# A state-space scan kernel in which GpSimd multiplies two channel tiles with one instruction

## The chip, the cores and the metric

The kernel runs on one core of one Trainium2 chip. The metric is the device time of one execution in microseconds (us); lower is better. The core has a tensor engine (PE in the profile, its weight loads PEld), a vector engine (DVE), a scalar engine (ACT), GpSimd (POOL) and a sync engine (SP) that issues most transfers. Each engine runs its own list of instructions in order, and they wait for each other through semaphores.

## The reference

An input `x` of 4 sequences of 1024 tokens with 256 features is layer-normalised to `xn`. Two things are made of `xn`: a mixture of 8 experts of which each token uses one, and a stack of 8 Mamba layers. The output is `x + s * silu(g)`, with `s` from the Mamba stack and `g` from the experts. The change lies in the Mamba layers, whose core is this recurrence over time, for 512 channels and 16 states:

```python
def _mamba_layer(x, Wi, cw, cb, Wx, Wdt, bdt, Alog, Dp, Wo):
    xz = jnp.einsum('bld,ed->ble', x, Wi)
    xin, z = jnp.split(xz, 2, axis=-1)
    xin = _silu(_causal_conv(xin, cw, cb))
    x_dbl = jnp.einsum('blc,ec->ble', xin, Wx)
    ...
    delta = jax.nn.softplus(jnp.einsum('blr,cr->blc', dt_raw, Wdt) + bdt)
    A = -jnp.exp(Alog)
    y = _selective_scan(delta, Bm, Cm, xin, A, Dp)
    y = y * _silu(z)
    return jnp.einsum('blc,dc->bld', y, Wo)

def step(h, inp):          # one token of _selective_scan
    d_t, B_t, C_t, u_t = inp
    h = h * jnp.exp(d_t[..., None] * A) + (d_t * u_t)[..., None] * B_t[:, None, :]
    y = jnp.einsum('bcn,bn->bc', h, C_t)
    return (h, y)
```

The term `(d_t * u_t) * B_t` is the drive of the recurrence. It is what the change is about.

## The kernel before

**Stages.** `experts` normalises and runs the mixture, `mamba` runs the 8 layers, `finish` combines both. `mamba` takes nearly the whole time.

**Units and tiles.** `mamba` works in 64 units: 8 layers times 4 sequences times 2 halves of 512 tokens. Channels lie on the 128 partitions, so the 512 channels are 4 tiles (index `j`), and time runs along the free dimension. A unit loops over 16 states (`n`) and the 4 channel tiles, which makes 64 tiles of 128x512 float32, numbered `k = 4n + j`. Units with even number U hold the first half of a sequence and start their states at 0; odd ones start them from `carry`, the last column of the unit before.

**One tile.** For tile `k`
- ACT (`exponent`, L784) writes the decay `exp(delta * A)` to `ps_d`, two buffers in PSUM;
- GpSimd (L743) writes `drive[k % 8] = du[j] * brep[n]`. `du` (`delta * u`, 4 tiles) is made once per unit by DVE in two instructions of two tiles each (`make_du`, L978, after tiles 58 and 63 of the unit before). `brep` is B of one state, spread over all partitions by a DMA, with 4 buffers;
- DVE (`scan`, L930) runs the recurrence over the 512 tokens with one TENSOR_TENSOR_SCAN of `ps_d` (in PSUM) and `drive` (in SBUF);
- PE transposes the state (L1085), ACT weighs it with C (L791, `prod`), PE transposes it back and adds it into `ps_y` (L1092).

**What holds GpSimd back.** The semaphore `scanned` counts scans and `drive_set` counts tiles of drive. There are 8 drive buffers, so tile `k` may be written once scan `k - 8` has ended (`scanned >= 64 U + k + 1 - DRIVE`, L742). Between the drives GpSimd has small work at fixed places: `keep_carry` (in even units after tile 4n + 9, waits for scan 4n + 3), `set_taps` after tile 16, `halo` after tile 17 (waits for the convolution step that DVE does after scan 14), `set_cur` after tile 20, `mask_x` (L705, two rows of 512 at once, one operand repeated) after tile 23, `set_skip` (L722, four small instructions) after tile 30.

**What DVE does between the scans.** The order is written out by hand as pairs (n, j), "after the scan of this tile": `CONV_AT`, `SOFT_AT`, `DU_AT`, `MARK_AT`, `ALIVE_AT`, `ADD_AT`. As tile numbers of the unit:
- convolution, 16 steps (L965 the first of each four, L969 the others): after tiles 7, 9, 12, 14, 14, 30, 33, 37, 39, 46, 47, 50, 52, 55, 59, 63; L965 is at 9, 30, 46 and 55;
- softplus, 8 steps of two tiles each: L988 after 27 and 35, L991 after 28 and 42, L995 after 29 and 60, L998 after 31 and 61;
- `make_du` (L978) after 58 and 63;
- marks of overflow: L939 after 6, L941 after 8; a scan of them (L952) after 10;
- `gate` (L1028) after tiles 4 to 7 and `add_x` (L1034) after 14 and 15, with one operand in PSUM each.

**PE and ACT.** Besides the transposes PE runs the projections, through a ring of two PSUM banks whose order is written out in `RING_AT`. ACT does both SiLUs of a unit after tile 15 (`SILU_AT`).

Of the kernel before, what the change touches and what calls it, by code (L numbers as in the profile page):

```python
# [27 lines left out]
ALU = mybir.AluOpType  # L28
# [3 lines left out]
P = 128  # L32
# [3 lines left out]
T = 512  # L36
# [32 lines left out]
TILES = STATES * CB  # L69
XD = RANK + 2 * STATES  # L70
BREP = 4
DRIVE = 8
# [410 lines left out]
def items_before(U, kind):  # L483

    if kind == "mid":
        every, vec = U * len(ITEMS["mid"]) + PRE_ALL, U * len(BY_DVE["mid"]) + PRE_DVE
        return every, vec, U * (len(ITEMS["mid"]) - len(BY_DVE["mid"])) + PRE_ALL - PRE_DVE
    past = ORDER[:ORDER.index(kind)]
    every, vec = sum(len(ITEMS[k]) for k in past), sum(len(BY_DVE[k]) for k in past)
    return every, vec, every - vec  # L490
# [22 lines left out]
def item_read(U, kind, name):  # L513

    i = ITEMS[kind].index(name)
    act, vec = reads(U, kind, i + 1)
    return vec if name in VEC_ITEMS else act
# [13 lines left out]
def mamba(nc, w_in, w_x, w_dt, w_out, par, xres, ident, alive_dram, bc_dram):  # L531

    with ExitStack() as ctx:
# [31 lines left out]
        du = sb("du", [P, CB, T])  # L565

        brep = sb("brep", [P, BREP, T])
        drive = sb("drive", [P, DRIVE, T])
# [20 lines left out]
        drive_set, decay_set, scanned, carried = sem("drive_set"), sem("decay_set"), sem("scanned"), sem("carried")  # L589
# [3 lines left out]
        def is_first(U):  # L593
            return isinstance(U, int) and U == 0

        def units(eng, unit):

            unit(0, 0, 0, "first")
            unit(1, 1, 0, "mid")
            with nc.Fori(1, ITERS - 1, 1, engines=[eng.engine], hint_back_edge=True) as it:  # L600
                for h in range(HALVES):
                    unit(HALVES * it + h, h, it, "mid")
            unit(UNITS - 2, 0, ITERS - 1, "near")
            unit(UNITS - 1, 1, ITERS - 1, "last")
# [76 lines left out]
        @block.gpsimd  # L681
        def _(pool):
            def wait_counted(semaphore, count):

                pool.wait_ge(semaphore, count)
                pool.sem_inc(pool_waited, 1)

            def set_cur(F, h, it):

                if not (isinstance(F, int) and F < 2):  # L690
                    wait_counted(scanned, TILES * (F - 1))
                nc.gpsimd.tensor_copy(cur[h][:], params[:, bass.ds(it // BATCH, 1), :].rearrange("p a c -> p (a c)")).then_inc(cur_set, 1)

            def set_taps(G, h, it):

                if not (isinstance(G, int) and G < 2):
                    wait_counted(conv_done, CB * (G - 1))
                nc.gpsimd.tensor_copy(taps[h][:], params[:, bass.ds(it // BATCH, 1), COL_W:COL_DT].rearrange("p a c -> p (a c)")).then_inc(taps_set, 1)

            def mask_x(U, kind, G, h, it):  # L700
                pool.wait_ge(ring_vec, item_read(U, kind, "CNT"))
                if not (isinstance(G, int) and G < 2):

                    pool.wait_ge(ring_ready, items_before(U, kind)[0])
                nc.gpsimd.tensor_tensor(xm[h][:], xres[:, :, bass.ds((it % BATCH) * SEQ + h * T, T)],  # L705
                                        alive[h][:].unsqueeze(1).to_broadcast([P, DB, T]), ALU.mult).then_inc(xm_set, 1)

            def halo(F, h):

                wait_counted(conv_done, CB * F + CB)  # L710
                if h == 0:
                    nc.gpsimd.tensor_copy(xpad[:, :, 0:TAPS - 1], xpad[:, :, T:T + TAPS - 1]).then_inc(halo_set, 1)
                else:
                    nc.gpsimd.memset(xpad[:, :, 0:TAPS - 1], 0.0).then_inc(halo_set, 1)

            def set_skip(F, h):

                if not is_first(F):
                    wait_counted(skip_used, F)
                wait_counted(cur_set, F + 1)  # L720
                for j in range(CB):
                    last = nc.gpsimd.tensor_scalar(skip[:, j, :], ident[:], cur[h][:, COL_D + j:COL_D + j + 1], 1.0,  # L722
                                                   ALU.mult, ALU.mult)
                last.then_inc(skip_set, 1)

            def keep_carry(U, n):

                wait_counted(scanned, TILES * U + CB * n + CB)
                nc.gpsimd.tensor_copy(carry[:, n, :], state[n % 2][:, :, T - 1]).then_inc(carried, 1)  # L729

            def unit(U, h, it, kind):
                F, hf, itf = U + 1, 1 - h, it + h
                G, itg = U + 2, it + 1
                for n in range(STATES):
                    for j in range(CB):
                        k = CB * n + j
                        if j == 0:
                            pool.wait_ge(brep_in[n % BREP], 16 * (STATES // BREP * U + n // BREP + 1))
                        if n == 0 and j % 2 == 0:
                            pool.wait_ge(du_set, 2 * U + j // 2 + 1)  # L740
                        if not (is_first(U) and k < DRIVE):
                            pool.wait_ge(scanned, TILES * U + k + 1 - DRIVE)  # L742
                        nc.gpsimd.tensor_tensor(drive[:, k % DRIVE, :], du[:, j, :], brep[:, n % BREP, :],  # L743
                                                ALU.mult).then_inc(drive_set, 1)
                        if h == 0 and k >= CARRY_LAG and k % CB == CARRY_LAG % CB:
                            keep_carry(U, (k - CARRY_LAG) // CB)
                        if h == 1 and k + TILES - CARRY_LAG < TILES and (k + TILES - CARRY_LAG) % CB == 0:
                            keep_carry(U - 1, (k + TILES - CARRY_LAG) // CB)
                        if kind != "last":
                            if (n, j) == CUR_AT:  # L750
                                set_cur(F, hf, itf)
                            if (n, j) == HALO_AT:
                                halo(F, hf)
                            if (n, j) == SKIP_AT:
                                set_skip(F, hf)
                        if kind in ("first", "mid"):
                            if (n, j) == TAPS_AT:
                                set_taps(G, h, itg)
                            if (n, j) == XM_AT:
                                mask_x(U, kind, G, h, itg)  # L760

            nc.gpsimd.memset(xdbl[:], 0.0).then_inc(xdbl_clear, 1)
            nc.gpsimd.memset(xpad[:, :, 0:TAPS - 1], 0.0).then_inc(halo_set, 1)
            pool.wait_ge(par_set, 1)
            set_cur(0, 0, 0)
            set_taps(0, 0, 0)
            set_taps(1, 1, 0)
            mask_x(0, "pre0", 0, 0, 0)
            set_skip(0, 0)
            halo(0, 0)  # L770
            mask_x(0, "pre1", 1, 1, 0)
            units(pool, unit)

        @block.scalar
# [590 lines left out]
```

## Time and profile before

| | |
|---|---|
| median of 3 runs | 8067.98 us (8058.57 to 8072.14) |
| the profiled execution | 8078.57 us, its span 8076.8 us |
| DVE busy | 85% of the span |
| PE busy | 84% |
| ACT busy | 80% |
| GpSimd (POOL) busy | 76% |
| tensor engine's mean granted clock | 0.971 of full |

The profiled execution is 0.13% above the median. Its span runs from the first to the last instruction, and 1.8 us of its time lie outside. All durations in this document come from that one execution unless a comparison of runs is named. An engine's "busy" time includes the time that an instruction, once issued, spends blocked.

### The profile page before, as it was taken

To read this page: it belongs to the slowest core of one execution; us is meant where nothing else is said; L and a number is where in the kernel's file an instruction comes from. 1 tells how busy PE (TensorE), PEld (TensorE's weight loads), DVE (VectorE), ACT (ScalarE), POOL (GpSimd) and SP (SyncE) were. 2 spreads that over 40 slices of the span, in tenths; PEclk is the share of its full clock that TensorE was granted. 3 is DMA by queue.
4 is the path that set the end of the run, shared out by engine and by line. 5 is a ranking of instruction groups with operands and counts; after the bars stand their busy time and mean duration, and the time that the engine had idled before them with its cause. 6 is when DMAs were issued, how large, how long until landed. Compare 5 with 4: busy or idle time off the path is not lost. (4 is left out here: it accounts for less than half of the span.)

```text
span 8076.8 us, 143189 instructions
## 1 busy us (share of the span) xinstructions
PE 6817.6 (84%) x39539; PEld 4773.9 (59%) x39539; DVE 6885.2 (85%) x6710; ACT 6451.8 (80%) x10242; POOL 6100.4 (76%) x5283
## 2 busy tenths in 40 slices
PE   4978888888888888888888888888888888888887
PEld 3645655655665656556555655665565566556655
DVE  2249889988988898889889988988998898889888
ACT  1248888888888888888888888888888888888886
POOL 2137877887888788888877887887788778878875
PEclk9989999999999999999999999999999999999998
DMA  5111111111111111111111111111111111111112
GB/s 167 34 33 38 38 35 44 41 38 37 41 40 40 38 38 41 42 38 38 38 42 40 38 38 38 41 40 36 37 44 41 38 37 40 41 39 38 37 37 88
DMA packets 205422, 348.52 MB, mean 43 GB/s; under 512 B 24976, under 2 KB 63664, under 8 KB 204496
## 3 DMA queue, kind: packets, MB, share of 16 engines
q1 hardware_dynamic: 201216, 329.67, 15.2%
q0 software_dynamic: 3408, 9.33, 0.3%
q8 instruction: 364, 5.96, 0.3%
q14 instruction: 434, 3.56, 0.1%
HBM read 318.04 MB, written 20.88 MB: 42 GB/s over the span
## 5 line engine op out<-in xcount | busy, mean ns | idle before, releaser
L743 POOL TENSOR_TENSOR drive<-du,brep 128x512 f32<-128x512 f32 x4096 | 5610.7, 1396 | 856.1 <-DVE du L978 641.1
L784 ACT ACTIVATE ps_d<-delta,cur 128x512 f32<-128x512 f32 x4096 | 2827.0, 690 | 867.1 <-DVE state L930 846.3
L1085 PE MATMUL ps_r<-ident,state 128*128 128x128 f32 x16384 | 2575.0, 281 | 565.1 <-ACT prod L791 338.6
L791 ACT ACTIVATE prod<-ps_r,bcT 128x512 f32<-128x512 f32 x4096 | 2784.7, 680 | 262.5 <-PE ps_r L1085 250.8
L930 DVE TENSOR_TENSOR_SCAN state<-ps_d,carry,drive 128x512 f32<-128x512 f32 x2048 | 2518.9, 1265 | 274.9 <-ACT ps_d L784 138.1
L930 DVE TENSOR_TENSOR_SCAN state<-ps_d,drive 128x512 f32<-128x512 f32 x2048 | 2394.1, 1205 | 280.2 <-ACT ps_d L784 139.4
L1092 PE MATMUL ps_y<-ident,prod 128*128 128x128 f32 x16384 | 2508.6, 278 | 27.6 <-ACT prod L791 25.4
L1085 PEld LDWEIGHTS ps_r<-ident,state 128*128 128x128 f32 x16384 | 1867.4, 143 | 878.3 <-ACT prod L791 558.0
L1092 PEld LDWEIGHTS ps_y<-ident,prod 128*128 128x128 f32 x16384 | 1960.3, 143 | 694.5 <-issue 489.1
L1125 PE MATMUL ps_r<-xm,w_inx_sb 128*128 128x512 f32 x1024 | 534.3, 648 | 189.6 <-ACT prod L791 181.9
L969 DVE SCALAR_TENSOR_TENSOR xc<-xpad,taps,xc 128x512 f32<-128x512 f32 x768 | 657.4, 856 | 2.9
L1133 PE MATMUL ps_r<-xm,w_inz_sb 128*128 128x512 f32 x1024 | 510.0, 621 | 126.0 <-ACT prod L791 125.8
L1162 PE MATMUL ps_r<-relu,w_out_sb 128*128 128x512 f32 x1024 | 471.6, 604 | 5.6 <-ACT prod L791 3.0
L1125 PEld LDWEIGHTS ps_r<-xm,w_inx_sb 128*128 128x128 f32 x1024 | 180.2, 195 | 384.3 <-issue 198.5
L1155 PE MATMUL ps_r<-xdbl,w_dt_sb 16*128 16x512 f32 x512 | 299.9, 666 | 84.2 <-ACT soft L837 51.4
L1133 PEld LDWEIGHTS ps_r<-xm,w_inz_sb 128*128 128x128 f32 x1024 | 174.6, 190 | 312.7 <-ACT prod L791 169.1
L729 POOL COPY carry<-state 128x4 f32<-128x4 f32 x512 | 189.7, 371 | 182.1 <-DVE state L930 179.6
L1162 PEld LDWEIGHTS ps_r<-relu,w_out_sb 128*128 128x128 f32 x1024 | 185.3, 191 | 202.2 <-issue 189.0
L1103 PE MATMUL ps_y<-u,skip 128*128 128x512 f32 x512 | 283.8, 692 | 23.5 <-DVE relu L1028 23.5
L1141 PE MATMUL ps_r<-u,w_x_sb 128*48 128x512 f32 x512 | 234.9, 602 | 54.4 <-ACT u L809 54.4
L425 ACT ACTIVATE hid<-ps_t,b_sb 128x128 f32<-128x128 f32 x312 | 84.8, 382 | 227.4 <-PE ps_t L386 227.4
L353 POOL DMA_INDIRECT ys_dram<-yb,row x39 | 37.2, 955 | 294.4 <-DVE yb L445 294.4
(136 smaller groups left out, 4471.4 us busy)
## 6 DMA issues: line engine op xcount, KB each, us to landing
brep<-bc_dram SPq DMA_DIRECT2D x1024, 256.0 KB, 3.3
w_sb<-w SPq DMA_DIRECT2D x8, 1024.0 KB, 17.9
w_all<-w SPq DMA_DIRECT2D x8, 1024.0 KB, 13.0
xs_dram<-nothing SPq DMA_DIRECT2D x1, 5011.5 KB, 35.0
xb<-xs_dram SPq DMA_DIRECT2D x39, 128.5 KB, 2.0
w_all<-x SPq DMA_DIRECT2D x1, 4096.0 KB, 14.7
w_inx_sb<-w_in SPq DMA_DIRECT2D x8, 512.0 KB, 4.0
w_inz_sb<-w_in SPq DMA_DIRECT2D x8, 512.0 KB, 4.0
```

The lines of the kernel that those rows point to most:

```text
L743: nc.gpsimd.tensor_tensor(drive[:, k % DRIVE, :], du[:, j, :], brep[:, n % BREP, :], ALU.mult).then_inc(drive_set, 1)
L784: nc.scalar.activation(ps_d[:, k % 2, :], delta[h][:, j, :], ACT.Exp, scale=cur[h][:, a:a + 1]).then_inc(decay_set, 1)
L791: nc.scalar.activation(prod[:, t, :], ps_r[:, item_place(U, h, kind, item), :], ACT.Copy, scale=bcT[(h + 1) % 2 if item[1] == "prev" else ...
L930: nc.vector.tensor_tensor_scan(state[n % 2][:, j, :], ps_d[:, k % 2, :], drive[:, k % DRIVE, :], carry[:, n, j:j + 1] if h == 1 else 0.0, ...
L969: step = nc.vector.scalar_tensor_tensor(xc[:, j, :], xpad[:, j, tap:tap + T], w, xc[:, j, :], ALU.mult, ALU.add)
L1085: last = nc.tensor.transpose(out[:, j * P:(j + 1) * P], state[n % 2][:, j, t * P:(t + 1) * P], ident[:])
L1092: last = nc.tensor.matmul(ps_y[:, j, t * P:(t + 1) * P], prod[:, t, j * P:(j + 1) * P], ident[:], start=False, stop=True, is_transpose=Tru ...
L1103: last = nc.tensor.matmul(ps_y[:, j, :], skip[:, j, :], u[:, j, :], start=True, stop=True, skip_group_check=True)
L1125: last = nc.tensor.matmul(out, w_inx_sb[:, k, j * P:(j + 1) * P], xm[h][:, k, :], start=(k == 0), stop=(k == DB - 1))
L1133: last = nc.tensor.matmul(out, w_inz_sb[:, k, j * P:(j + 1) * P], xm[hf][:, k, :], start=(k == 0), stop=(k == DB - 1))
L1155: nc.tensor.matmul(out, w_dt_sb[:, j * P:(j + 1) * P], xdbl[0:RANK, :], start=True, stop=True).then_inc(ring_ready, 1)
L1162: last = nc.tensor.matmul(out, w_out_sb[:, j, k * P:(k + 1) * P], gated[:, j, :], start=(j == 0), stop=(j == CB - 1))
```

## The change

GpSimd makes the products of channel tiles `j` and `j + 1` (for even `j`) with one TENSOR_TENSOR of 2 x 512 elements per partition. Its second operand, the row of `brep`, is repeated for both with stride 0. There are 32 such instructions per unit in place of 64. Each waits until both of its buffers are free, and counts `drive_set` up by 2 when it ends. The small work of GpSimd keeps its places in the loop, so what stood between two tiles of a pair now stands behind the pair.

```diff
--- before.py
+++ after.py
@@ -738,10 +738,11 @@
                             pool.wait_ge(brep_in[n % BREP], 16 * (STATES // BREP * U + n // BREP + 1))
                         if n == 0 and j % 2 == 0:
                             pool.wait_ge(du_set, 2 * U + j // 2 + 1)
-                        if not (is_first(U) and k < DRIVE):
-                            pool.wait_ge(scanned, TILES * U + k + 1 - DRIVE)
-                        nc.gpsimd.tensor_tensor(drive[:, k % DRIVE, :], du[:, j, :], brep[:, n % BREP, :],
-                                                ALU.mult).then_inc(drive_set, 1)
+                        if j % 2 == 0:
+                            if not (is_first(U) and k < DRIVE):
+                                pool.wait_ge(scanned, TILES * U + k + 2 - DRIVE)
+                            nc.gpsimd.tensor_tensor(drive[:, k % DRIVE:k % DRIVE + 2, :], du[:, j:j + 2, :],
+                                                    brep[:, n % BREP:n % BREP + 1, :].to_broadcast([P, 2, T]), ALU.mult).then_inc(drive_set, 2)
                         if h == 0 and k >= CARRY_LAG and k % CB == CARRY_LAG % CB:
                             keep_carry(U, (k - CARRY_LAG) // CB)
                         if h == 1 and k + TILES - CARRY_LAG < TILES and (k + TILES - CARRY_LAG) % CB == 0:
```

## Rows read from the trace of the kernel before

**Rows 1.** The page: the span and each engine's busy time.
```profile
span 8076.8 us, 143189 instructions
PE 6817.6 (84%) x39539; PEld 4773.9 (59%) x39539; DVE 6885.2 (85%) x6710; ACT 6451.8 (80%) x10242; POOL 6100.4 (76%) x5283
```

**Rows 2.** The waits over the span: us in total, times, longest.
```profile
POOL drive L743 <- DVE du L978: 641.1, 126, 7.2
...
DVE state L930 <- ACT ps_d L784: 277.5, 199, 6.1
...
POOL drive L743 <- DVE state L930: 154.0, 145, 4.7
...
DVE state L930 <- POOL drive L743: 42.1, 26, 1.8
```

**Rows 3.** One line's instructions each: duration in ns, min/median/max; six lines.
```profile
L743 POOL TENSOR_TENSOR drive<-du,brep x4096: 1250/1274/2293, 531.7 to 8001.4; 128x512 f32<-128x512 f32 x196
...
L705 POOL TENSOR_TENSOR xm<-xres,alive x64: 2337/2370/2394, 476.5 to 7727.0; 128x1024 f32<-128x1024 f32 x64
...
L969 DVE SCALAR_TENSOR_TENSOR xc<-xpad,taps,xc x768: 717/799/1844, 484.0 to 7834.5; 128x512 f32<-128x512 f32 x192
...
L965 DVE TENSOR_SCALAR xc<-xpad,taps x256: 514/598/1602, 483.4 to 7826.2; 128x512 f32<-128x512 f32 x128
...
L991 DVE TENSOR_TENSOR low<-soft,low x128: 1192/1399/3756, 509.4 to 7887.1; 128x1024 f32<-128x1024 f32 x128
...
L1028 DVE TENSOR_TENSOR relu<-ps_y,zs x256: 657/666/693, 671.2 to 8016.1; 128x512 f32<-128x512 f32 x128
```

**Rows 4.** Timeline of POOL in an even unit: start, us, what.
```profile
4096.39 4.99 POOL L743 TENSOR_TENSOR drive<-du,brep 128x512 f32<-128x512 f32 x4
...
4110.40 3.72 POOL L743 TENSOR_TENSOR drive<-du,brep 128x512 f32<-128x512 f32 x3
4116.41 2.17 POOL L743 TENSOR_TENSOR drive<-du,brep 128x512 f32<-128x512 f32 x1 [2.30 <-DVE state L930]
```

**Rows 5.** Timeline of DVE in the same unit.
```profile
4111.46 3.74 DVE L991 TENSOR_TENSOR low<-soft,low 128x1024 f32<-128x1024 f32 x1
...
4116.25 1.19 DVE L995 TENSOR_TENSOR low<-low,delta 128x1024 f32<-128x1024 f32 x1
...
4136.53 1.53 DVE L991 TENSOR_TENSOR low<-soft,low 128x1024 f32<-128x1024 f32 x1
4137.98 4.55 DVE L930 TENSOR_TENSOR_SCAN state<-ps_d,drive 128x512 f32<-128x512 f32 x4
4142.46 1.07 DVE L965 TENSOR_SCALAR xc<-xpad,taps 128x512 f32<-128x512 f32 x1
```

**Rows 6.** Timeline of DVE in the odd unit behind it.
```profile
4189.73 1.52 DVE L965 TENSOR_SCALAR xc<-xpad,taps 128x512 f32<-128x512 f32 x1
...
4253.58 1.39 DVE L991 TENSOR_TENSOR low<-soft,low 128x1024 f32<-128x1024 f32 x1
4254.89 4.79 DVE L930 TENSOR_TENSOR_SCAN state<-ps_d,carry,drive 128x512 f32<-128x512 f32 x4
4259.61 0.65 DVE L965 TENSOR_SCALAR xc<-xpad,taps 128x512 f32<-128x512 f32 x1
```

**Rows 7.** Timeline at the change of units: DVE.
```profile
4170.41 1.20 DVE L978 TENSOR_TENSOR du<-delta,u 128x1024 f32<-128x1024 f32 x1
4171.53 0.74 DVE L969 SCALAR_TENSOR_TENSOR xc<-xpad,taps,xc 128x512 f32<-128x512 f32 x1
4172.19 4.80 DVE L930 TENSOR_TENSOR_SCAN state<-ps_d,carry,drive 128x512 f32<-128x512 f32 x4
```

**Rows 8.** The same moment: POOL.
```profile
4171.77 5.32 POOL L743 TENSOR_TENSOR drive<-du,brep 128x512 f32<-128x512 f32 x4 [6.90 <-DVE du L978]
```

**Rows 9.** Windows, an even and an odd unit: us, then each engine's busy time.
```profile
4055.40:4171.50 116.10, 101.20 (x597) 70.18 (x596) 104.54 (x100) 99.04 (x155) 94.38 (x87) 0.97 0.16 43
4171.50:4288.00 116.50, 100.27 (x592) 70.48 (x590) 104.87 (x100) 98.51 (x155) 94.12 (x73) 0.97 0.14 38
```

## The prediction

> **What bounds the kernel now.** I read the page first: no engine is full; DVE is busiest with 85%, GpSimd has 76% [rows 1]. The windows of two neighbouring units say that a unit takes 116.3 us, of which DVE is busy 104.5 to 104.9 and GpSimd 94 [rows 9]. The waits come next. GpSimd waits 641 us for `du`, about 10 us per unit, and 154 us for scans; DVE waits for a drive in only 26 places, 42 us in all [rows 2]. So GpSimd runs ahead, and making it faster shortens no wait that DVE has for it. DVE's own large wait is for the decay, 277.5 us [rows 2]; it falls after the two SiLUs, between tiles 15 and 26. From tile 27 to 63, and from 0 to 14, DVE works nearly without a gap. There DVE sets the pace: a microsecond more in one of its instructions is a microsecond more per unit.
>
> The third view, durations by line, holds what decides. `gate` (one operand in PSUM) takes 657 to 693 ns always, while L969, L965 and L991 go from 717, 514 and 1192 ns to 1844, 1602 and 3756 [rows 3]. The timelines of both engines show why. L991 is issued at 4111.46, inside a run of three drives that ends at 4114.12. It ends at 4115.20, so its own 1.19 us began at 4114.01, when those drives were over [rows 3 to 5]. The reverse stands 2 us later: L995 is issued at 4116.25, a drive at 4116.41; the drive takes 2.17 us and ends 1.13 us behind L995's end of 4117.44 [rows 4, 5]. So a DVE instruction with two operands in SBUF, or a TENSOR_SCALAR out of SBUF, and a GpSimd product exclude each other, and the later one waits until the earlier is over. Scans, gates and `add_x`, with an operand in PSUM, don't wait. I call the others port instructions; a unit has 28 of them (16 of the convolution, 8 softplus, 2 `du`, 2 marks).
>
> Here is what the wait costs now. A wait is a duration less the line's minimum. In the even unit I find 0.2 to 0.6 us at single places (0.34 on L991 after tile 42, 0.56 on L965 after tile 46) [rows 3, 5], and 2.55 once, after tile 28, where L991 sat through three drives. Over the whole unit that is 6.1 us. In the odd unit it is 2.9 us, of which 1.0 after tile 9 and 0.2 on L991 after tile 42 [rows 3, 6]. They are so small because the lengths fit: a drive takes 1.25 us (four in 4.99) [rows 4], a scan 1.12 us from start to start in even units (four in 4.48) [rows 5] and 1.18 in odd ones (4254.89 to 4259.61) [rows 6]. When DVE comes back for the port after one, two or three scans, a drive is just ending.
>
> **The change part by part.**
>
> *Fewer, longer instructions.* The trace has one of the new form, `mask_x`: 1024 elements, one operand repeated, 2.37 us [rows 3]. Two drives in a row take 2.50 [rows 4]. So a pair costs 2.37, with two drives as the upper bound, and GpSimd saves 0.13 x 32 = 4 us per unit. This is worth nothing by itself: it goes into GpSimd's waits for scans.
>
> *Both buffers must be free.* Pair (k, k+1) waits for scan k-7, an odd one. It is ready about 2.4 us later, while scan k is 6 scans (over 6.7 us) away. This is free in the steady part. Carry copies stay behind the same tiles and in time.
>
> *Start of a unit.* The pair (2, 3) can't start before the second `du`. Today GpSimd starts at 4171.77, is blocked by L969 until 4172.27, and makes four drives until 4177.09; scans 0 and 1 run from 4172.19 [rows 7, 8]. New: the pair ends about 2.2 us after 4172.27, at 4174.5. Scan 2 wants it at 4172.19 + 2 x 1.18 = 4174.55 in odd units, and 0.1 us earlier in even ones. I take 0, bound 0.2 us; the cover is scans 0 and 1.
>
> *The port.* This is the term that counts. GpSimd now waits for odd scans, so in the full part of the unit it starts a pair when an odd scan ends and keeps the port over the next two scans (2.37 us against 2.24 or 2.36). A port instruction behind an odd tile comes just as the pair ends: DVE goes first, wait 0 to 0.2. One behind an even tile comes in the middle of a pair. It waits 2.37 - 1.12 (or 1.18), less some 0.1 for the early hand-over, so 1.1; where the pair itself was late or a copy came before it, up to 1.4. Behind even tiles stand 6, 8, 12, 14, 14, 28, 30, 42, 46, 50, 52, 58, 60. At 12 and 14 GpSimd is idle before `halo`, at 58 and 60 it waits for `du`; after 59 the pair (0, 1) of the next unit, started by the first `du`, is in the way. I walked both kinds of unit from scan to scan:
> - Even unit, new waits: after 6 0.75, 7 0.4, 8 1.3, 27 0.3, 28 1.15, 30 1.1, 33 and 37 0.15 each, 42 1.3, 46 1.45, 50 1.3, 52 1.3, 55 0.1, 59 1.0. Sum 11.75, less today's 6.1: +5.65. After 28 it gains: GpSimd has only one pair allowed there, not three drives.
> - Odd unit: after 6 0.65, 7 0.3, 8 0.95, 9 0, 27 0.1, 28 and 30 0.95 each, 42 and 46 1.15 each, 50 and 52 1.1 each, 55 0.1, 59 1.0. Sum 9.5, less 2.9: +6.6.
>
> Mean 6.1 us per unit, times 64: 390 us. DVE's idle time in these parts that could soak it up is 0.2 us per unit, left out. PE and ACT have more slack when DVE slows. Against the profiled span that is 8076.8 + 390 = 8467. The median of the runs lies 10 us under the profiled execution: 8068 + 390 = 8458, I say 8460.
>
> The Trainium skill (SBUF — State Buffer, "Who interferes with whom") states that GpSimd and such DVE instructions share a port pair as an exclusive lock, held for the whole instruction. By that rule a 1024-element product blocks for all its length, which is the case forecast here, 8460; a port that came free between the two rows would give the first rival's 8010 instead. The trace agrees for 512 elements; no run here yet shows it for 1024 elements. The wait over three drives [rows 4, 5] is longer than that rule alone gives.
>
> **Rivals.**
> - *Faster: the port comes free between the two rows of a pair.* Then waits at single places stay near today's 0.2 to 0.6 us, and the one of 2.55 us after tile 28 falls, as GpSimd may be only one pair ahead there. It decides if the mean port wait at even tiles stays under 0.4 us. Price: -1.4 to -2.5 us in 32 even units, -45 to -80: 8010. For it speaks only that `mask_x` never met a port instruction, so 1024 elements aren't seen. Chance 0.08.
> - *Nothing moves:* the waits shift but sum up alike, within 0.2%: 8068. With 6 to 7 even places per unit it would take chance. 0.04.
> - *Only the late pair:* the port is as the first rival has it, and DVE waits at the start of each unit for a pair that ends one drive later: 1.1 us x 64 = 70, 8140. Against it stands that DVE waits for a drive only 42 us today, and scans 0 and 1 cover. Chance 0.06.
> - *DVE loses the port more often.* After tile 28 it asked 0.1 us before a drive ended and lost two further hand-overs. With pairs and scans nearly equally long such close calls may come at each odd tile (27, 33, 37, 55). Each costs a whole pair, 2.3 us x 64 = 147 us: 8610 with one per unit, 8750 with two. Against it: at most odd tiles GpSimd isn't yet allowed its next pair. Chance 0.12.
> - *My forecast*, 0.70: own range 8320 to 8560. The low end has the even places at 0.7 of my wait (4 us per unit, +255); the high end adds a lost hand-over in every second or third unit.
>
> **How the numbers follow.** The time is the likeliest case's, 8460. The range leaves out the cases at or under 8140 (0.18) and the top of the last rival (0.03): 8200 to 8640. A measurement of this kernel can tell about 0.2% (16 us) from no change. Slower by more: 0.70 + 0.12 + 0.06 = 0.88; within: 0.04; faster: 0.08.
>
> **What would show it.** In the profile after: L743 x2048 at 2.37 us minimum, GpSimd's unblocked work down, its waits for scans up from 154 us; L991 at two clear lengths, near 2.1 to 2.5 after tiles 28 and 42; L965 after 30 and 46 at 1.4 to 2.0 and after 9 and 55 at 0.5 to 0.7; L969 after 50 and 52 near 1.9; L941, 0.66 today, near 1.6 to 2.0; scans and gates unchanged; the unit 122 to 123 us. I am wrong if L965 and L969 keep their medians, if a unit's DVE gains idle time for drives of over 0.5 us, or if pairs take more than 2.5 us unblocked.

## The result and the profile after

The changed kernel takes 8469.06 us (median of 4 runs, 8461.93 to 8473.27) against 8070.06 us of the kernel before in the same comparison. The ratio is 1.0495, 95% interval 1.0476 to 1.0513: 4.9% slower. The profiled execution has a span of 8471.5 us. In the changed kernel's file the lines behind L743 are one higher: the product is L744, the scan L931, the convolution L966 and L970, softplus L989, L992, L996 and L999, the marks L940 and L942.

First the page, its span and busy times, beside [rows 1]:

```profile
span 8471.5 us, 141141 instructions
PE 6905.9 (82%) x39475; PEld 4785.2 (56%) x39539; DVE 7284.9 (86%) x6710; ACT 6467.2 (76%) x10242; POOL 5572.9 (66%) x3235
```

GpSimd is 527 us less busy with its products in 2048 instructions, DVE is 400 us more busy with the same 6710 instructions. The span grew by 395 us. So the time sits inside DVE's instructions, not between them. Five of the six lines of [rows 3], duration in ns as min/median/max, and the second mark (L942, after tile 8):

```profile
L744 POOL TENSOR_TENSOR drive<-du,brep x2048: 2340/2367/3205, 528.4 to 8396.2; 128x1024 f32<-128x1024 f32 x187
...
L970 DVE SCALAR_TENSOR_TENSOR xc<-xpad,taps,xc x768: 715/742/2721, 478.4 to 8228.5; 128x512 f32<-128x512 f32 x192
...
L966 DVE TENSOR_SCALAR xc<-xpad,taps x256: 514/636/2035, 477.8 to 8220.3; 128x512 f32<-128x512 f32 x128
...
L992 DVE TENSOR_TENSOR low<-soft,low x128: 1225/2290/2698, 506.1 to 8283.1; 128x1024 f32<-128x1024 f32 x128
...
L942 DVE TENSOR_SCALAR over_mark<-xres x64: 683/1658/1868, 466.5 to 8090.8; 128x1024 bf16 x60, 128x1024 bf16<-128x1024 f32 x4
...
L1029 DVE TENSOR_TENSOR relu<-ps_y,zs x256: 656/664/693, 671.6 to 8412.5; 128x512 f32<-128x512 f32 x128
```

A pair takes 2.37 us, as forecast. Note the convolution: its median fell from 799 to 742 ns, while its maximum rose. Most of its steps stand behind odd tiles and wait less than before; a few wait a whole microsecond more. A median alone would have hidden the loss, and the prediction's sign "wrong if L965 and L969 keep their medians" was a poor one for that reason: they went from 598 to 636 and from 799 to 742 ns. The gate, with an operand in PSUM, is unchanged.

The place decides, and the timeline of DVE in an even unit shows it (tiles 37 to 47: start, us, what):

```profile
4076.86 0.74 DVE L970 SCALAR_TENSOR_TENSOR xc<-xpad,taps,xc 128x512 f32<-128x512 f32 x1
4077.53 2.32 DVE L931 TENSOR_TENSOR_SCAN state<-ps_d,drive 128x512 f32<-128x512 f32 x2
4079.77 0.72 DVE L970 SCALAR_TENSOR_TENSOR xc<-xpad,taps,xc 128x512 f32<-128x512 f32 x1
4080.42 3.43 DVE L931 TENSOR_TENSOR_SCAN state<-ps_d,drive 128x512 f32<-128x512 f32 x3
4083.78 2.56 DVE L992 TENSOR_TENSOR low<-soft,low 128x1024 f32<-128x1024 f32 x1
4086.26 4.55 DVE L931 TENSOR_TENSOR_SCAN state<-ps_d,drive 128x512 f32<-128x512 f32 x4
4090.74 2.03 DVE L966 TENSOR_SCALAR xc<-xpad,taps 128x512 f32<-128x512 f32 x1
4092.70 1.21 DVE L931 TENSOR_TENSOR_SCAN state<-ps_d,drive 128x512 f32<-128x512 f32 x1
4093.83 0.72 DVE L970 SCALAR_TENSOR_TENSOR xc<-xpad,taps,xc 128x512 f32<-128x512 f32 x1
```

And GpSimd at the same time:

```profile
4080.51 4.75 POOL L744 TENSOR_TENSOR drive<-du,brep 128x1024 f32<-128x1024 f32 x2
4087.64 0.19 POOL L729 COPY carry<-state 128x4 f32<-128x4 f32 x1 [2.38 <-DVE state L931]
4087.79 4.70 POOL L744 TENSOR_TENSOR drive<-du,brep 128x1024 f32<-128x1024 f32 x2
```

Behind the odd tiles 37, 39 and 47 the convolution takes 0.72 to 0.74 us. L992 follows tile 42: issued at 4083.78, it ends at 4086.34, so its own 1.19 us began at 4085.15, 0.1 us before the second pair ended at 4085.26. L966 follows tile 46 and ends at 4092.77, so its own 0.51 us began at 4092.26, 0.23 us before the pairs ended at 4092.49. And GpSimd now idles, because pairs wait for scans (the waits, us in total, times, longest; beside [rows 2]):

```profile
POOL drive L744 <- DVE state L931: 895.1, 683, 7.8
POOL drive L744 <- DVE du L979: 692.7, 124, 8.9
...
DVE state L931 <- ACT ps_d L785: 286.7, 195, 6.1
```

The forecast went place by place, so it can be checked so. Waits in us, the mean over units 5 to 61 of the duration less the line's minimum in the kernel before. The table has the port instructions with 0.15 us or more somewhere, and the sum is that of all:

```
even unit, after tile    6    7    8   27   28   30   33   37   42   46   50   52   59   sum
before                 .59  .58    0  .36 1.98  .12  .27  .17  .34  .56  .29  .38  .22   6.20
forecast               .75  .40 1.30  .30 1.15 1.10  .15  .15 1.30 1.45 1.30 1.30 1.00  11.75
after                  .67  .40 1.20  .26  .98  .94  .03  .03 1.36 1.51 1.29 1.46 1.37  11.72

odd unit, after tile     6    7    8    9   27   28   30   42   46   50   52   59        sum
before                   0  .49    0 1.01  .26    0    0  .20  .14  .13    0  .16        3.07
forecast               .65  .30  .95    0  .10  .95  .95 1.15 1.15 1.10 1.10 1.00        9.50
after                  .48  .34  .99    0  .14  .91  .88 1.30 1.19 1.23 1.24 1.31       10.12
```

A unit lasts 123.48 us in place of 117.00 (means over the same units). The waits make 6.3 us of the 6.5. The first five units and the last two grow by less, so the span grows by 395 us and not by 64 x 6.5 = 415.

### The profile page after: what moved, and what is told of

Same layout as the page of the kernel before. It is cut to its first block and busy times, and to the rows that moved or that the text cites. A ratio compares the mean times of both kernels' runs of the same rounds, so it can differ in the third digit from the quotient of the medians.

```text
span 8471.5 us, 141141 instructions
## 1 busy us (share of the span) xinstructions
PE 6905.9 (82%) x39475; PEld 4785.2 (56%) x39539; DVE 7284.9 (86%) x6710; ACT 6467.2 (76%) x10242; POOL 5572.9 (66%) x3235
## 5 line engine op out<-in xcount | busy, mean ns | idle before, releaser
L744 POOL TENSOR_TENSOR drive<-du,brep 128x1024 f32<-128x1024 f32 x2048 | 5062.6, 2481 | 1609.3 <-DVE state L931 895.1
L931 DVE TENSOR_TENSOR_SCAN state<-ps_d,carry,drive 128x512 f32<-128x512 f32 x2048 | 2519.6, 1265 | 255.4 <-ACT ps_d L785 134.2
L931 DVE TENSOR_TENSOR_SCAN state<-ps_d,drive 128x512 f32<-128x512 f32 x2048 | 2398.0, 1204 | 304.9 <-ACT ps_d L785 152.5
L970 DVE SCALAR_TENSOR_TENSOR xc<-xpad,taps,xc 128x512 f32<-128x512 f32 x768 | 834.5, 1087 | 2.9
L1134 PE MATMUL ps_r<-xm,w_inz_sb 128*128 128x512 f32 x1024 | 542.6, 656 | 192.7 <-ACT prod L792 192.4
L992 DVE TENSOR_TENSOR low<-soft,low 128x1024 f32<-128x1024 f32 x128 | 296.4, 2316 | 0.1
L966 DVE TENSOR_SCALAR xc<-xpad,taps 128x512 f32<-128x512 f32 x256 | 276.3, 1079 | 13.7 <-ACT xpad L798 13.7
```

Of the source, the lines that this page charges most:

```text
L744: nc.gpsimd.tensor_tensor(drive[:, k % DRIVE:k % DRIVE + 2, :], du[:, j:j + 2, :], brep[:, n % BREP:n % BREP + 1, :].to_broadcast([P, 2, T ...
L931: nc.vector.tensor_tensor_scan(state[n % 2][:, j, :], ps_d[:, k % 2, :], drive[:, k % DRIVE, :], carry[:, n, j:j + 1] if h == 1 else 0.0, ...
L970: step = nc.vector.scalar_tensor_tensor(xc[:, j, :], xpad[:, j, tap:tap + T], w, xc[:, j, :], ALU.mult, ALU.add)
L992: nc.vector.tensor_tensor(low[:], soft[:, pair, :], low[:], ALU.subtract).then_inc(soft_step, 1)
L1134: last = nc.tensor.matmul(out, w_inz_sb[:, k, j * P:(j + 1) * P], xm[hf][:, k, :], start=(k == 0), stop=(k == DB - 1))
```

## The experiments

All compare with runs of the kernel before on the same chip. The theory is the one of the prediction: GpSimd's product and DVE's port instructions exclude each other, and a port instruction that meets a pair in its middle waits for its end.

**e1: two halves.** The pair's wait stays, its product becomes two instructions:

```diff
-    nc.gpsimd.tensor_tensor(drive[:, k % DRIVE:k % DRIVE + 2, :], du[:, j:j + 2, :], ...).then_inc(drive_set, 2)
+    nc.gpsimd.tensor_tensor(drive[:, k % DRIVE, :], du[:, j, :], brep[:, n % BREP, :], ALU.mult).then_inc(drive_set, 1)
+    nc.gpsimd.tensor_tensor(drive[:, k % DRIVE + 1, :], du[:, j + 1, :], brep[:, n % BREP, :], ALU.mult).then_inc(drive_set, 1)
```

> The pair's wait (both buffers free) is kept, but its product is made by two instructions of 512 elements, one right behind the other. Port theory: DVE can take the port between the halves, so the waits of the port instructions fall from the changed kernel's 1.0 to 1.4 us behind even tiles back to 0.1 to 0.4; 7980 to 8100 us. Rival, the coarse signal (GpSimd starts later because two buffers must be free, and drives come later): the time stays near the changed kernel's 8470, at least above 8350.

Measured: 8102.63 us, ratio 1.0047 (1.0030 to 1.0064), 2.6 us above the top of the theory's interval and far from the rival's 8350. Its convolution and L992 (here L971 and L993), by line:

```profile
L971 DVE SCALAR_TENSOR_TENSOR xc<-xpad,taps,xc x768: 718/752/1639, 483.4 to 7861.0; 128x512 f32<-128x512 f32 x192
...
L993 DVE TENSOR_TENSOR low<-soft,low x128: 1198/1530/2509, 508.7 to 7912.8; 128x1024 f32<-128x1024 f32 x128
```

The waits after 42, 46, 50 and 52 are back at 0.34, 0.56, 0.29 and 0.38 us in even units, to the hundredth those of the kernel before. Elsewhere e1 isn't the kernel before: 1.0 us more after tile 30 in both kinds of unit and 0.9 more after 28 in odd ones, 1.5 less after 28 in even ones. Summed, its waits are 5.2 and 4.5 us per unit against 6.2 and 3.1, which is 0.2 us more in the mean; another 0.2 is idle time of DVE, before tiles 23 and 24. So of the 399 us some 360 belong to the length of the instruction, and some 40 to the later start. The rival falls.

**e2: the other phase.** Each pair waits for one scan more and starts when an even scan ends:

```diff
-    pool.wait_ge(scanned, TILES * U + k + 2 - DRIVE)
+    pool.wait_ge(scanned, TILES * U + k + 3 - DRIVE)
```

> The changed kernel, each pair waiting for one scan more, so that GpSimd starts it when an even scan ends. Port theory: what decides is where a port instruction falls within the pair. Behind even tiles (42, 46, 50, 52) the waits fall from over 1.0 to below 0.3 us, behind odd ones (27, 29, 31, 33, 35, 37, 39, 47, 55) they rise from 0 to 0.2 to about 1.1; more places are odd than even in that stretch, so 8450 to 8600 us. Rival, the longer instruction costs its wait at random, whatever the phase: the same places keep their waits and the time stays within 0.3% of 8470.

Measured: 8676.87 us, ratio 1.0751 (1.0733 to 1.0768), 77 us above the top of the theory's interval. The direction and the places are its own. L999 follows tiles 31 (in the way of a pair now) and 61 (not), and its two durations part:

```profile
L999 DVE TENSOR_TENSOR delta<-low,relu x128: 1191/1224/2575, 511.9 to 8517.1; 128x1024 f32<-128x1024 f32 x128
```

In even units the waits after 42, 46, 50 and 52 fall from 1.3 to 1.5 us to 0.24, 0.14, 0.18 and below 0.1; those after 29, 31, 33, 35, 37, 39 and 55 rise from below 0.15 to 1.05 to 1.35. Against the expectation, after 27 it is 0.2 us and not 1.1; after 28 it stays at 1.1. The waits of a unit sum to 3.3 us more than in the changed kernel, and the unit is 3.3 us longer. The same instruction at the same length costs 200 us more or less, by its phase alone.

**e8: the cost doubled.** From the second state on one product of 4 x 512 elements:

```diff
-    if j % 2 == 0: ... pool.wait_ge(scanned, TILES * U + k + 2 - DRIVE) ... [P, 2, T] ... .then_inc(drive_set, 2)
+    w = 2 if n == 0 else 4
+    if j % w == 0: ... pool.wait_ge(scanned, TILES * U + k + w - DRIVE) ... [P, w, T] ... .then_inc(drive_set, w)
```

> The suspected cost doubled: from the second state on, one product of 4 x 512 elements, started when a scan 4m+3 ends and 4.7 us long. Port theory: a port instruction waits 3.4 us behind a tile 4m, 2.3 behind 4m+1, 1.2 behind 4m+2, 0 to 0.2 behind 4m+3; L991 after 28 takes 4.6, L969 after 33 and 37 3.0, after 52 4.1, L998 after 31 1.2. With some idle time for late drives 9000 to 9300 us. Rival, a port instruction waits at most for one row of 512 or a fixed time: 8500 or less.

Measured: 9361.17 us, ratio 1.161 (1.1591 to 1.1629), 61 us above the interval. The product's median (2048 elements) and the convolution's maximum:

```profile
L745 POOL TENSOR_TENSOR drive<-du,brep x1088: 2343/4537/5387, 528.1 to 9280.7; 128x2048 f32<-128x2048 f32 x160, 128x1024 f32<-128x1024 f32 x22
...
L971 DVE SCALAR_TENSOR_TENSOR xc<-xpad,taps,xc x768: 718/1659/4871, 480.4 to 9111.3; 128x512 f32<-128x512 f32 x192
```

The waits in even units are 3.5 us after 52 (tile 4m), 2.1 and 2.0 after 33 and 37 (4m+1), 1.0, 1.2 and 0.9 after 42, 46 and 50 (4m+2), about 0 after 35, 39 and 55. The expectation had 3.4, 2.3, 1.2 and 0 to 0.2. After 28 it is 2.75, less than expected, and after 7 4.0, where 0 to 0.2 was expected. A port instruction waits for the rest of whatever product is running. The waits of a unit sum to about 21.6 and 20.7 us, some 16.5 more than in the kernel before in the mean; the unit is 20.7 us longer, and most of the rest is idle time of DVE (3.9 us, 1.2 of it before the gate of tile 4).

**e5: four instructions moved by one tile.** The changed kernel with L992 of tile 42 behind 43, and the convolution of 46, 50 and 52 behind 45, 51 and 53:

```diff
-CONV_AT = [..., (11, 2), (11, 3), (12, 2), (13, 0), ...]
+CONV_AT = [..., (11, 1), (11, 3), (12, 3), (13, 1), ...]
-SOFT_AT = [(6, 3), (7, 0), (7, 1), (7, 3), (8, 3), (10, 2), (15, 0), (15, 1)]
+SOFT_AT = [(6, 3), (7, 0), (7, 1), (7, 3), (8, 3), (10, 3), (15, 0), (15, 1)]
```

> The changed kernel with four port instructions moved by one tile, from behind tiles 42, 46, 50 and 52 to 43, 45, 51 and 53, nothing else. Their waits in the changed kernel sum to 5.6 us per even and 5.0 per odd unit. Port theory: these waits go almost wholly (0 to 0.1 left each), no others come, 64 x 5.0 = 320 us: 8150, between 8120 and 8200. Rival after e3, the waits only hide ACT's and PE's own limit and come back as DVE's idle time: 8300 or more.

Measured: 8165.06 us, ratio 1.0126 (1.0109 to 1.0143), 15 us from the forecast. Four entries in a table take back 300 of the 400 us. 0.25 us is left after 43, 0.19 after 51 in even units, 0.13 or less in odd ones.

**e3 and e4: all of them odd.** All port instructions of tiles 27 to 63 stand behind odd tiles, the marks both behind 7; e3 with pairs, e4 with the kernel before's products:

```diff
-CONV_AT = [(7, 2), (8, 1), (9, 1), (9, 3), (11, 2), (11, 3), (12, 2), (13, 0), (13, 3), (14, 3), (15, 3), ...
-DU_AT = [(14, 2), (15, 3)]
+CONV_AT = [(9, 1), (9, 3), (10, 1), (11, 1), (11, 3), (12, 1), (12, 3), (13, 1), (13, 3), (14, 1), (14, 3), ...
+DU_AT = [(14, 3), (15, 3)]
-MARK_AT, ALIVE_AT, ADD_AT = [(1, 2), (2, 0)], ...
-SOFT_AT = [(6, 3), (7, 0), (7, 1), (7, 3), (8, 3), (10, 2), (15, 0), (15, 1)]
+MARK_AT, ALIVE_AT, ADD_AT = [(1, 3), (1, 3)], ...
+SOFT_AT = [(6, 3), (7, 1), (7, 3), (8, 1), (8, 3), (10, 3), (15, 1), (15, 1)]
```

> The changed kernel, with DVE's port instructions of tiles 27 to 63 and the two marks moved behind odd tiles (which scan each follows, nothing else). Port theory: all of them then come as a pair ends, their waits sum to 1 to 2.5 us per unit in place of 10.6 and fall below those of the kernel before (4.5), so 7830 to 7950 us, faster than both kernels. Rival, pairs are too coarse for DVE in any order (lost hand-overs, a drive that comes late): 8200 or more, with waits of over 1 us behind odd tiles too. A convolution or softplus step that now comes too late for ACT or PE would show as new idle time of DVE at tiles 0 to 26.

> The kernel before (64 products of 512 elements) with DVE's instructions at the same odd places as e3: the control for e3. Port theory: with drives of 1.25 us against scans of 1.12 or 1.18 two scans fall 0.15 to 0.25 us short of two drives, so each place waits 0.1 to 0.3 us, a sum of 3 to 5 us, as before; the wait of 2.55 us at tile 28 may vanish. 7980 to 8070 us, so e3 beats it by 1% or more. Rival, the moved places alone make the gain: e4 is as fast as e3 within 0.3%.

Measured: e3 8218.64 us (1.0191, 1.0174 to 1.0208), e4 8240.84 (1.0222, 1.0205 to 1.0239). Both expectations missed, e3 by 269 us and e4 by 171, counted from the top of each interval; e3's time is that of its rival. What the theory says of the places came true: behind all odd tiles from 29 to 63 e3 has waits below 0.1 us, and only 0.26 and 0.14 after 27. What undid it stands elsewhere. The three port instructions behind tile 7 wait 3.4 us together in even units and 3.2 in odd ones; DVE then idles 1.1 us before the scan of marks at tile 10 and 0.4 to 0.8 before tile 12; and 0.8 to 1.5 us of new idle time stands before tiles 31 and 32. e4 shares the waits behind tile 7 (2.3 and 3.2 us) and the idle time before tiles 10 and 12 (1.5 us together), but has only 0.3 to 0.4 before 31 and 32, and waits 2.0 us after 29 in even units. The two lie 0.3% apart, so with these places pairs and single products lose alike: the places made this loss, if not by the same waits in both.

**e6 and e7: near the old places.** Fewer moves: L992 28 to 29 (where L996 stands already), L966 30 to 31 (where L999 stands), the convolution of 59 to 57, four moved as in e5, the marks behind 1 and 3; e6 with pairs, e7 without.

```diff
+CONV_AT = [(7, 3), (8, 1), (9, 1), (9, 3), (11, 1), (11, 3), (12, 3), (13, 1), (13, 3), (14, 1), (15, 3), ...
+MARK_AT, ALIVE_AT, ADD_AT = [(0, 1), (0, 3)], ...
+SOFT_AT = [(6, 3), (7, 1), (7, 1), (7, 3), (8, 3), (10, 3), (15, 0), (15, 1)]
```

> Pairs, with each port instruction behind an odd tile or where GpSimd idles, but close to its old place, so that tiles 27 to 31 aren't thinned out as in e3: four moved as in e5, L991 28 to 29, L965 30 to 31, the convolution of 59 to 57, the marks to tiles 1 and 3, where DVE idles 0.8 us before the first gate. Port theory: 10 to 11 us per unit less than the changed kernel, 7780 to 7850. Rival (ACT and PE take over as limits): idle time of DVE before the scans of tiles 28 to 40 grows by over 1 us per unit and the time stays above 7950.

> The kernel before with DVE's instructions at the places of e6: its control. Port theory: singles keep waits of 0.1 to 0.3 us at most places, some 3 us per unit, and save the marks' idle time: 7900 to 8020, above e6. If it ties with e6 the longer instruction is worth nothing even where it fits.

Measured: e6 8330.35 us (1.0333, 1.0316 to 1.0350), e7 8114.09 (1.0063, 1.0046 to 1.0080). Both missed, e6 by 480 us and e7 by 94, counted from the top of each interval. e6 didn't miss by its rival's way: there is no new idle time before tiles 28 to 40. The timeline of DVE shows what I had done (odd unit, two port instructions behind tile 29, two behind 31):

```profile
4100.70 1.20 DVE L992 TENSOR_TENSOR low<-soft,low 128x1024 f32<-128x1024 f32 x1
4101.94 3.27 DVE L996 TENSOR_TENSOR low<-low,delta 128x1024 f32<-128x1024 f32 x1
4105.12 2.45 DVE L931 TENSOR_TENSOR_SCAN state<-ps_d,carry,drive 128x512 f32<-128x512 f32 x2
4107.49 1.19 DVE L999 TENSOR_TENSOR delta<-low,relu 128x1024 f32<-128x1024 f32 x1
4108.61 2.59 DVE L966 TENSOR_SCALAR xc<-xpad,taps 128x512 f32<-128x512 f32 x1
```

and of GpSimd:

```profile
4100.93 3.19 POOL L744 TENSOR_TENSOR drive<-du,brep 128x1024 f32<-128x1024 f32 x1 [0.39 <-DVE state L931]
4107.71 3.20 POOL L744 TENSOR_TENSOR drive<-du,brep 128x1024 f32<-128x1024 f32 x1 [3.59 <-DVE state L931]
```

The pair issued at 4100.93 waits for L992, which ends at 4101.90, and then takes the port before L996: L996's own 1.19 us began at 4104.02, as the pair ended at 4104.12. So two neighbouring port instructions don't keep the port; the second pays for a whole pair, 2.1 us. Two more losses in e6 have no such neighbour: 1.8 us after tile 7 in both kinds of unit (0.4 and 0.3 in the changed kernel), and 2.1 on the mark after tile 1 in odd ones. Behind tile 7 the gate comes first. A pair that had waited for a scan was issued at 4296.01, during that gate, and the convolution step only at 4296.37.

**e9: e3 with the marks back at tiles 6 and 8.**

```diff
-MARK_AT, ALIVE_AT, ADD_AT = [(1, 3), (1, 3)], ...
+MARK_AT, ALIVE_AT, ADD_AT = [(1, 2), (2, 0)], ...
```

> e3 with the two marks back at tiles 6 and 8, nothing else. In e3 three port instructions follow each other behind tile 7 and wait 3.4 and 3.2 us together, DVE then idles 1.1 us before the scan of marks (tile 10) and 0.6 before tile 12. Theory: neighbours on one tile lose the port to a waiting pair between them, and the marks came too late for PE; at 6 and 8 they cost the 1.8 to 2.3 us of waits they cost in the changed kernel. 64 x 2.7 = 170 us less than e3's 8219: 8050, 8010 to 8090. Rival, the thinned stretch of tiles 27 to 33 is what holds e3 back: 8150 or more.

Measured: 8056.91 us (median of 10), 1.0 thousandth under the kernel before (0.9990, 0.9980 to 0.9999), 7 us from the forecast. Its convolution and L992:

```profile
L970 DVE SCALAR_TENSOR_TENSOR xc<-xpad,taps,xc x768: 716/735/2717, 480.9 to 7811.3; 128x512 f32<-128x512 f32 x192
...
L992 DVE TENSOR_TENSOR low<-soft,low x128: 1192/1198/1587, 508.6 to 7864.4; 128x1024 f32<-128x1024 f32 x128
```

L992 hardly waits any more (median 1198 ns; 2290 in the changed kernel, 1399 before). Waits are 2.9 and 2.2 us per unit, less than the kernel before's 6.2 and 3.1. DVE's idle time is 2.0 and 0.7 us per unit higher and takes most of the gain. Some 1.4 to 1.5 us of new idle time stand before tiles 31, 32 and 39 in both kinds of unit, and 0.3 to 0.4 before tile 2, where DVE now waits for a drive; in odd units 1.2 us less before 23 and 24 make up for much of it.

**e10 and e11: the count of overflows moved to where DVE idles**, e10 on e3's places with pairs, e11 on the kernel before:

```diff
-RING_AT = {"CNT": (2, 1), ...
+RING_AT = {"CNT": (5, 0), ...
+MARK_AT, ALIVE_AT, ADD_AT = [(4, 1), (4, 1)], (5, 1), [(3, 2), (3, 3)]
-... XM_AT = ... (5, 3)
+... XM_AT = ... (6, 1)
```

> e3 with the count of overflows (two marks, PE's count, the scan of it) moved from tiles 6 to 10 to tiles 17 to 21, where DVE idles 8 us per unit for ACT and PE; mask_x moves from behind tile 23 to behind 25, and the store that follows the count comes later in SP's queue. Port theory: 2.0 us of waits and 2.5 us of DVE's own work leave the full stretch: 64 x 4 = 256 us less than e9's expected 8050: 7800, 7760 to 7880, clearly under the kernel before. Rival: those 8 us are a chain through ACT's SiLUs and the ring of PE, and work put there is not hidden: 8000 or more.

> The kernel before (64 products of 512 elements, its own places) with the count moved as in e10: the control for e10. The kernel before spends 0.3 us on waits of the marks and 2.5 on their work: 64 x 2.8 = 180 us less, 7890, 7850 to 7950. If pairs are worth anything when they fit DVE's order, e10 is 0.5% or more faster than e11; if e11 is as fast or faster, the longer product gains nothing in any order that I found.

Measured: e10 8267.47 us (1.0247, 1.0233 to 1.0261), e11 8259.51 (1.0240, 1.0226 to 1.0254). Both missed; the rival recorded for e10 (8000 or more) holds for both. They tie, so by what was recorded for e11 the longer product gains nothing here. The waits of e11:

```profile
POOL xm L705 <- DVE alive L952: 534.8, 54, 32.7
...
DVE alive L952 <- PE ps_r L1116: 223.3, 64, 4.8
```

DVE's idle time there isn't free room. It now waits 3 to 4 us per unit for PE's count, and GpSimd waits 10 us in 54 of the units for the marks' scan before `mask_x`. GpSimd comes out of that without its lead, and the port waits after 27 and 30 are 0.6 to 1.1 us each; that the lost lead is their cause wasn't tested. e11's waits sum to about 8 us per unit.

**e12: e9 with the marks behind tiles 3 and 5.**

```diff
+MARK_AT, ALIVE_AT, ADD_AT = [(0, 3), (1, 1)], ...
```

> e9 with the two marks behind tiles 3 and 5 in place of 6 and 8, nothing else. Port theory, walked as for the prediction: at tile 3 a pair has just ended (wait 0) and DVE idles 0.8 us before the gate of tile 4, which hides the mark's work; at tile 5 a pair is in the way for 0.6 us; the 1.7 us per unit that the marks wait in e9 go. Up to 0.5 us may come back at tile 7. 64 x 1.7 = 110 us less than e9's 8057: 7950, 7920 to 8010, faster than both kernels. Rival, GpSimd can't spare the port so near the start of the unit: the drives of tiles 4 and 6 come late, DVE's idle time there or at 10 grows by what the waits save, and the time stays at 8040 or more.

Measured: 8220.87 us (1.0196, 1.0181 to 1.0211), missed by 270 us. The mark behind tile 3 waits 2.2 us where I had 0. DVE and GpSimd there:

```profile
4008.51 2.46 DVE L931 TENSOR_TENSOR_SCAN state<-ps_d,carry,drive 128x512 f32<-128x512 f32 x2 [0.31 <-POOL drive L744]
4010.88 2.84 DVE L940 TENSOR_SCALAR over_mark<-xres 128x1024 bf16 x1
```

```profile
4010.67 0.19 POOL L729 COPY carry<-state 128x4 f32<-128x4 f32 x1
4010.82 7.42 POOL L744 TENSOR_TENSOR drive<-du,brep 128x1024 f32<-128x1024 f32 x3
```

The scan of tile 3 ends at 4010.97, the pair was issued at 4010.82. At the start of a unit GpSimd is behind and issues pairs back to back, so no odd scan sets its phase. The mark, issued at 4010.88, comes 0.06 us behind the pair and pays for all of it. The mark after tile 5 waits 1.2 and 0.9 us, and the convolution step after tile 7, again behind a gate, 2.0 and 1.8 in place of e9's 0.4 and 0.3. The idle time before the gate did hide (0.9 us per unit less), but the waits sum to 5.9 and 5.3 us per unit against e9's 2.9 and 2.2.

## Why the prediction was right

**GpSimd's speed is worth nothing.** Right. The products' busy time fell from 5611 to 5063 us, GpSimd's waits for scans rose from 154 to 895 us, and nothing came of it.

**Both buffers free, the start of a unit.** Right in size: e1 has the same coarse wait and is 0.5% above the kernel before, and its remainder is port waits and idle time for ACT and PE, not drives that came late. DVE's list of waits after the change has none for a drive above 16 us in all.

**The port term.** Right, to 0.03 us per even unit and 0.6 per odd one in the sums. The largest misses at single places are after 59, 1.0 forecast and 1.3 to 1.4 measured, and after 28 and 30, up to 0.2 too high. Part of the closeness is luck, since such misses cancel in the sums. So it is with the total: 390 us forecast, 399 measured between the medians. The growth per unit was forecast 0.4 us too low (6.1 against 6.5), which is 23 us over 64 units, and 64 units are some 20 us too many at that rate, since the first and last grow less. The range would have held either error alone. e1 takes the long instruction away and some 360 us of it go; e2 and e5 move the phase or the places and the waits follow; e8 doubles the length and they double. The shared port that the Trainium skill describes (SBUF — State Buffer, "Who interferes with whom"), held for the whole instruction, is borne out for 1024 and 2048 elements by these waits (1.3 us after tile 42, 3.5 after 52 in e8).

**What the working read wrongly.** Two small terms didn't matter. It took the unit as 116.3 us from two windows and forecast 122 to 123; over units 5 to 61 the means are 117.00 and 123.48. And it gave DVE 0.2 us of idle time per unit outside tiles 15 to 26; the trace of the kernel before has 1.7 us there in even units and 1.0 in odd ones, mostly before the gate of tile 4. The changed kernel took up 0.3 us of it in even units and none in odd ones.

**The rivals.** A port free between the rows falls with the 1.3 us after tile 42 and with e8. The late pair alone falls with e1. Lost hand-overs, which I gave 0.12, did not come in the changed kernel; but they are real, as e3, e6 and e12 show, and are a large part of why these three missed; e10 and e11 missed by waits for PE's count. "DVE goes first at an odd tile" held only where GpSimd was waiting for that scan, and for one instruction right behind it. Where GpSimd had the next pair already issued, or a gate or another port instruction came between, it didn't. The rival's case for it, the 2.55 us after tile 28, has a wrong number: DVE asked 0.2 us before a drive's end there, not 0.1.

**What stays open.** In e3 and e9 DVE's new idle time before tile 31 ends with ACT's decay and that before 32 with PE; what holds those two up wasn't taken apart. Nor was e9 run with single products and its marks, so its 0.1% isn't shown to come from the pairs. The misses of e3, e4 and e6 are explained by waits read at their places. That neighbours were the cause in e3 was tested once, by e9, which also brought the marks forward for PE, so the two causes weren't parted. e4 waits 2.0 us after tile 29 without a neighbour, in even units, and e7 2.5 and 1.1 us there with one; neither was followed up.

## What to carry to other kernels

Before making GpSimd's instructions longer, list the VectorE instructions with two operands in SBUF, or a TENSOR_SCALAR out of SBUF, and ask of each where in GpSimd's instruction it falls: the rest of that instruction is its price, and a faster GpSimd buys nothing if it already waits for VectorE. Where GpSimd is paced by a semaphore, the phase is fixed and the price can be worked out place by place. Keep GpSimd's instructions short where such uses are many (with the pair's wait, products of 512 and 1024 elements made 8103 and 8469 us here, and 2048 elements 9361), don't put two such uses side by side or behind a gate, and read durations by place, since a line's median can fall while its sum rises.

## What the runs showed of the hardware that I had not expected

- A waiting DVE instruction gets the port 0.1 to 0.2 us before the product's end in the profile: 4085.15 against 4085.26 and 4104.02 against 4104.12 for softplus, 4092.26 against 4092.49 for a first step of the convolution.
- DVE may ask before a product's end and still lose the hand-over: 2.55 us over three drives [rows 4, 5]. After tile 28 of the kernel before it asked 0.19 to 0.21 us ahead of a drive's end and lost in 20 units; after 42 it asked 0.3 us ahead and got the port at that end. And GpSimd takes the port between two neighbouring DVE instructions (e6, 2.1 us).
- GpSimd's product has little fixed cost: medians of 1.27, 2.37 and 4.54 us for 512, 1024 and 2048 elements. By these medians two drives made into one save 0.18 us of its time (0.13 against two in a row, 2.50), a quad 0.2 against two pairs.
